# Moving the steps' adjacency loads from the SyncE queue to the ScalarE queue in a masked attention kernel

## The reference

```
h      = maximum(layernorm(x), 0)
scores = where(adj > 0, (h @ weight) @ nodes.T, -2**32 + 1)
out    = x + softmax(scores / 0.07, axis=1) @ nodes
```

## Time and profile before

| | us |
|---|---|
| median of three runs | 947.19 |
| the profiled execution's own time | 949.89 |
| its span | 948.1 |
| TensorE busy (PE) | 919.0 (97%) |
| VectorE busy (DVE) | 815.1 (86%) |
| ScalarE busy (ACT) | 760.7 (80%) |
| GpSimd busy (POOL) | 618.6 (65%) |
| queue q1 (SyncE), share of 16 DMA engines | 97.4% |
| queue q10 (ScalarE), share of 16 DMA engines | 1.2% |

### The profile page before, as it was taken

One profiled execution on the slowest core, in us unless ns is written; L12 is line 12 of the kernel. 1 busy time (PEld: TensorE's weight loads), 2 busy tenths in 40 slices (PEclk: granted clock), 3 DMA queues, 4 the chain that ended last, 5 costly groups with the idle time before them and its releaser, 6 DMA issues.

```text
span 948.1 us, 25836 instructions
## 1 busy us (share of the span) xinstructions
PE 919.0 (97%) x7611; PEld 666.1 (70%) x7611; DVE 815.1 (86%) x1670; ACT 760.7 (80%) x1517; POOL 618.6 (65%) x437
## 2 busy tenths in 40 slices
PE   6788999999999999999999999999999999999997
PEld 4356667777777777777777777777777777777776
DVE  5887889888889888889888889888889888889885
ACT  4676688888888888888888888888888888888886
POOL 1875667766777676677667677766776676677620
PEclk9989999999999999999999999999999999999999
DMA  9777999999999999999999999999999999999955
GB/s 284 251 188 199 216 286 268 270 270 251 262 274 262 266 267 266 257 268 270 264 257 266 265 267 265 271 266 252 268 266 269 265 260 269 260 268 268 266 100 98
DMA packets 351977, 239.51 MB, mean 253 GB/s; under 512 B 308816, under 2 KB 333520, under 8 KB 333520
## 3 DMA queue, kind: packets, MB, share of 16 engines
q1 hardware_dynamic: 345040, 236.05, 97.4%
q10 hardware_dynamic: 6912, 3.15, 1.2%
HBM read 160.50 MB, written 3.15 MB: 173 GB/s over the span
## 4 chain that ended last, share of the span: by engine, by line
PE 88%; DMA 1%; DVE 1%; SPq 1%; ACT 0%; issue 0%; DVEq 0%; ACTq 0%
PE ps_s L695 37%; PE ps_o L733 25%; PE ps_o L735 13%; PE ps_t L713 13%; DMA pT_dma<-split 1%; SPq L280 1%; PE ps_s L688 1%; DVE split L524 0%; DVE pT_lo L518 0%; ACT ps_t L392 0%; DVE probs L502 0%; ACT probs L383 0%; DVE fin_a L541 0%; ACT pT_hi L422 0%; DVE fin L547 0%
## 5 line engine op out<-in xcount | busy, mean ns | idle before, releaser
L502 DVE CUSTOM_DVE_ANT_0 probs<-ps_s,absent 128x1024 f32<-128x1024 f32 x288 | 351.4, 1220 | 85.1 <-PE ps_s L695 71.4
L343 POOL TENSOR_SCALAR absent<-adj_i 128x2048 bf16<-128x2048 int32 x143 | 270.6, 1893 | 213.4 <-DVE chunk_max L502 179.5
L347 POOL TENSOR_SCALAR absent<-absent 128x2048 bf16<-128x2048 bf16 x143 | 271.3, 1897 | 27.2 <-POOL absent L343 27.2
L422 ACT ACTIVATE pT_hi<-ps_t 128x512 f16<-128x512 f32 x288 | 171.8, 597 | 110.8 <-PE ps_t L713 108.1
L392 ACT ACTIVATE ps_t<-probs,neg_max,exp_scale 128x512 f32<-128x512 f32 x288 | 222.9, 774 | 2.8 <-DVE neg_max L512 1.5
L695 PE MATMUL ps_s<-yT_hi,hT_hi 128*128 128x512 f16 x576 | 219.6, 381 | 5.6 <-DVE chunk_max L502 4.9
L695 PE MATMUL ps_s<-yT_lo,hT_hi 128*128 128x512 f16 x576 | 219.5, 381 | 0.0
L733 PE MATMUL ps_o<-v,pT_dma 128*128 128x256 f16 x1152 | 206.3, 273 | 4.6 <-DVE v L562 3.2
L733 PE MATMUL ps_o<-v,pT_hi 128*128 128x256 f16 x1152 | 206.0, 273 | 2.2 <-DVE v L562 2.1
L518 DVE TENSOR_TENSOR pT_lo<-ps_t,pT_hi 128x512 f16<-128x512 f32 x288 | 196.5, 683 | 5.2 <-ACT pT_hi L422 5.2
L735 PE MATMUL ps_o<-v,pT_dma 128*128 128x128 f16 x1152 | 198.4, 219 | 0.0
(11 more groups left out here) (68 smaller groups left out, 584.3 us busy)
## 6 DMA issues: line engine op xcount, KB each, us to landing
adj_i<-in_adj_dram SPq DMA_DIRECT2D x144, 1024.0 KB, 5.3
pT_dma<-split SPq DMA_TRANSPOSE x288, 3.6
x_ln<-in_x_dram SPq DMA_DIRECT2D x48, 64.0 KB, 5.0
nodes_raw<-in_L_gnn_input_dram SPq DMA_DIRECT2D x4, 768.0 KB, 8.3
x_res<-in_x_dram SPq DMA_DIRECT2D x48, 64.0 KB, 4.9
out_dram<-fin ACTq DMA_DIRECT2D x48, 64.0 KB, 2.9
w<-in_L_gnn_weight_dram SPq DMA_DIRECT2D x1, 64.0 KB, 1.8
```

The costliest lines, as they stand in the source:

```text
L343: nc.gpsimd.tensor_scalar(absent[:, c, :], adj_i[:, c, :], 1.0, 0.0, ALU.min, ALU.max)\
L347: nc.gpsimd.tensor_scalar(absent[:, c, :], absent[:, c, :], -ABSENT, ABSENT, ALU.mult, ALU.add)\
L422: nc.scalar.activation(pT_hi[:, p % BANKS, :], ps_t[k % BANKS][:, :], ACT.Copy).then_inc(hi_done, 1)
L502: nc.vector.tensor_tensor_reduce(out=probs[:, s, j * SCORE:(j + 1) * SCORE], in0=ps_s[j % 2][:, :], in1=absent[:, c, part * SCORE:(part + ...
```

## The change

The three adjacency loads of a step leave SyncE's stream. ScalarE waits for `present_done` and issues the load of chunk z from its own hardware queue at the end of cycle z. The wait values, the buffers, the sizes and the semaphores are the same. The loads ahead of the steps, the DMA transposes and the loads of x stay with SyncE.

```
@@ SyncE, step
-                def next_adj(c):
-                    if has(at, 3):
-                        sp.wait_ge(present_done, t * CONVS + (2 * CONVS + c))
-                        load_adj(t + 3, c)
-
                 for g in range(2):
                     turn_d(t, 2, g, evac(t, g - 2))
-                next_adj(0)
                 for g in range(2):
                     turn_d(t, 4, g, evac(t, 2 + g))
-                next_adj(1)
                 if has(at, 4):
                     sp.wait_ge(h_done, t + 3)
                     load_x(t + 4, par)
                 if has(at, 1):
                     for g in range(2):
                         turn_d(t + 1, 0, g, evac(t, 6 + g))
-                next_adj(2)
@@ ScalarE
+            def next_adj(t, c):
+                act.wait_ge(present_done, t * CONVS + (2 * CONVS + c))
+                act.dma_start(adj_i[:, c, :], adj_v[t + 3][:, c * CONV:(c + 1) * CONV]).then_inc(adj_in[c], 16)
@@ ScalarE, end of cycle z in step
                     if at == 0 and z < 2:
                         v_hi(2 + z)
+                    if has(at, 3):
+                        next_adj(t, z)
```

## The result

The changed kernel takes 1020.8 us (median of 4 runs, 1012.5 to 1032.6) against 946.7 us in the same measurement. The ratio is 1.0747, 95% interval 1.0643 to 1.0851; it leaves out the run of 1032.6 us, which was in the chip's slower state. By the medians that is 74 us more, or 74 / 135 = 0.55 us for each of the 135 loads that moved; a cycle of TensorE grew from 6.19 to about 6.74 us on average.

The account below looks back on a forecast made before the run. The prediction took TensorE to bound the kernel. Steady stretch 0 for SyncE and 0 for ScalarE, head between -1.2 and +1.5 us, tail 0, summed to 0 us: 947.2 us, range 943.5 to 953.

Parts of the forecast that it names:

- What bounds the kernel: Whole span: TensorE bounds it, 88% of the chain, busy 760.00 of 760 us in the steady stretch; nothing to win there.
- rival B: Steady stretch: loads and transposes mix, transposes land later, TensorE's slack runs out; 970 us, at the bound 1001 us; 13%.
- What SyncE gives up: SyncE, three load issues per step of 0.34 to 0.37 us each: nothing waits on them, worth 0 us.
- What ScalarE takes on: ScalarE, 135 load issues behind the second `hi_d`: 0.17 us each, at most 0.66, hidden in idle time, 0 us.
- rival C: ScalarE's load issue held while SyncE generates descriptors, 1.4 us once per step; 949 us; chance 8%.
- When the data comes: GpSimd's conversions: cycle 0's load issued 1.2 us later, its chunk still landing 1.6 us before its conversion; 0 us.
- The transposes: DMA transposes ahead of `hi_d`: landing grows by -0.6 to +2.5 us, taken as +0.8; idle time absorbs it, TensorE unaffected.
- The 0.46 us of room: Cycle 0: time from the transpose's landing at 420.5 to the start of the second `hi_d` at 420.96.
- The page on queues: Skill page: DMA engines take packets in turn from queues; so load through first, transpose landing still between the two bounds.

Follow-up runs that it names:

- e9: e2 with six split buffers in place of three; 949.1 us, ratio 1.0014.
- e8: e2 with each load bringing only 1536 of 2048 columns; 1017.9 us, ratio 1.0756.
- e2: Kernel before the change, SyncE still issuing the loads, but each only after ScalarE's second `hi_d` of the cycle; 1095.5 us, ratio 1.1568.
- e4: Changed kernel with each load in the steps bringing only 1024 of 2048 columns; 947.3 us, ratio 0.9991.
- e1: Changed kernel with ScalarE issuing the loads earlier, between the two `exp_d` and the two `hi_d` of the cycle; 1034.7 us, ratio 1.0937.
- e5: Kernel before the change, SyncE issuing the load between the two transposes of a pair instead of behind both; 1011.5 us, ratio 1.0665.
- e6: Changed kernel with ScalarE issuing each load between its two `hi_d` of the cycle; 957.5 us, ratio 1.0131.

## Why the prediction was wrong, point by point

- **What bounds the kernel.** Right for the kernel before. The prediction says that "the DMA engines have no idle time" and, in the next sentence, against rival B, that the queue "empties every cycle". It draws nothing from either, and the share of 1.03 would not have decided: e9 has 1.03 and loses 0.14%, e8 has 0.83 and loses 7.6%, e2 has 0.85 and loses 15.7%. What counts is whether the path from one load to the next is longer than TensorE's cycle.
- **What SyncE gives up.** Its time is worth nothing, as forecast. What it gave up and I did not price is a place: directly behind the pair, early enough for the start-up of the load to hide behind the pair's data.
- **What ScalarE takes on.** Forecast 0.17 us; measured 515.00 - 514.27 = 0.73 us from `hi_d` to `hi_p`, against 0.50 without an issue, so 0.23 us. At 519.27, where the issue went out ahead of the `hi_d`, the distance is 0.48 us, so nothing. It was hidden (e4). No issue was held by SyncE's descriptor work: their median is 0.34 us and the longest 0.66 us, so rival C did not happen. The lock that the Trainium skill (Perfetto Trace Analysis, DMA Instruction — HWDGE) describes cost ScalarE nothing that these rows show. What grew was the issue of transposes on SyncE: from 140 to 900 us 89 of 225 took over 1.4 us, up to 4.80, where before it was 7 of 246. Why stays open; in e9 it was 122 of 245, and e9 took only 949.1 us.
- **When the data comes.** I had GpSimd with 1.6 us in hand. It waited 159.5 us for loads in the steady stretch. That is a consequence: with six buffers on e2, behind the same wait for `hi_d`, it waited 4.9 us.
- **The transposes.** This is the step that failed. I bounded the growth of the landing at -0.6 to +2.5 us and it was +2.3 us, inside; I took +0.8. But the sum after it, "0.8 + 0.17 - 0.34 = 0.6 us late at `hi_p(4)`", treated the delay as happening once, with idle time behind it to absorb it. The late `hi_d` is itself what the next load stands behind, so the delay is passed on to the next cycle, and where the ring closes it sets the period: 6.97 us in the cycle shown, 6.74 on average, against 6.19. I followed transpose, `hi_d`, `hi_p` and VectorE, and never `hi_d`, load, transpose. The data was there: second `hi_d` at 420.96, next transposes at 422.74, load behind the first and before the second. The 0.46 us of room was mis-sized too. It took the median of all transposes, 3.6 us; the one at 416.89 landed after 4.0 us, so at 420.9, less than 0.1 us ahead of the `hi_d` that needs it.
- **Rival B** named the right place and gave it the wrong mechanism. It priced +2.5 us at 1001 us, by slack used up 45 times. The measured 1020.8 us is 0.55 us on average in each of 135 cycles. Its chance of 13% and the top of the range, 953 us, rested on the same missing ring.
- **The page on queues.** From the Trainium skill (DMA: Bandwidth & Descriptors, Queues, rings and completion order) I took that packets of two queues alternate, and concluded that the load would be through first. In e1 between 506.5 and 508.0 us each queue moved 72 packets,

```profile
q10 hardware_dynamic: 72, 0.59, 93.8%
q1 hardware_dynamic: 72, 0.02, 5.4%
```

  one for one, which gives the load's 8 KB rows nearly all the time. There the trace agrees with the rule. But between 512.5 and 514.5 us in e1, and 508.5 and 512.0 us in the changed kernel, the load's queue moved alone while a transpose was issued and not landed; whether that transpose had packets ready then, no row shows. I used the rule only to bound a landing, and not to ask which transposes could now be overtaken.

## What to carry to other kernels

Before a transfer's issue is moved behind another instruction, ask what that instruction waits for, and whether that wait ends sooner or later with this very transfer; if the path closes, add up the whole ring (issue, start-up, data, landing, release) and compare it with the period. Do this even if the engine that issues is idle and the DMA share is well below 1 (0.83 in e8). Where the order of transfers matters, look at it again after the move: issued by one engine, their order in its stream set it (e2, e5); issued by two, only their issue times did, and 0.6 us earlier or later was a different program (e6, 957.5 against 1020.8 us).

## What the runs showed of the hardware that I had not expected

- Two DMA queues gave no order between a load and a transpose whose issue had begun 0.08 us ahead of it; the load's data went first (e1). With 0.5 to 1.3 us of lead it landed after 3.3 us (29 cases in the changed kernel), as in the kernel before.
- A load needs about 2 us from issue to full rate, whether it meets idle DMA engines (e2: issued at 509.39, 131 GB/s at 510.0, 377 at 511.5) or not (before: issued at 420.01, 344 GB/s from 422.0). Issued behind two transposes, their data fills most of that time.
- A pair of transposes on SyncE took 4.1 us to issue when a load had been issued 1.2 us and a small load of x 0.7 us ahead of it (e2), against 2.8 us.
